# Decoder layer on one core: the first tokens per tile, the first scores earlier, and a new order of weight splits

## The reference

```python
x = x + attention(layernorm(x))           # 16 heads of 64, keys and values from the same tokens
x = x + cross_attention(layernorm(x), ctx)# 16 heads of 16, keys and values from ctx, masked
x = x + experts(layernorm(x))             # 8 experts 256 -> 512 -> 256, gelu, summed and gated
```

## Time and profile before

| | |
|---|---|
| median of 3 runs | 907.7 us |
| the profiled execution's own time | 908.18 us |
| its span | 906.4 us |
| TensorE busy | 861.6 us (95%) |
| ScalarE busy | 626.7 us (69%) |
| VectorE busy | 562.3 us (62%) |
| GpSimd busy | 308.7 us (34%) |
| granted TensorE clock, mean | 0.991 |

### The profile page before, as it was taken

One profiled execution on the slowest core, in us unless ns is written; L12 is line 12 of the kernel. 1 busy time (PEld: TensorE's weight loads), 2 busy tenths in 40 slices (PEclk: granted clock), 3 DMA queues, 4 the chain that ended last, 5 costly groups with the idle time before them and its releaser, 6 DMA issues.

```text
span 906.4 us, 18085 instructions
## 1 busy us (share of the span) xinstructions
PE 861.6 (95%) x6299; PEld 781.1 (86%) x6299; DVE 562.3 (62%) x1167; ACT 626.7 (69%) x1772; POOL 308.7 (34%) x355
## 2 busy tenths in 40 slices
PE   8899999999999987999998799999999999999997
PEld 6798989989998976888888689999999999999996
DVE  5788898888889866787887755454223322332223
ACT  4988888888887865989898956754454445444542
POOL 4564564445455658465755520000000000000000
PEclk9999999999999997999999999999999999999999
DMA  5410000000000027555455113310000000000000
GB/s 179 146 41 1 2 1 1 2 1 2 1 25 1 2 55 184 127 149 132 103 140 140 48 52 102 94 34 24 1 1 1 24 0 0 0 24 1 1 1 24
DMA packets 21792, 42.29 MB, mean 47 GB/s; under 512 B 3144, under 2 KB 3152, under 8 KB 21712
## 3 DMA queue, kind: packets, MB, share of 16 engines
q1 hardware_dynamic: 21120, 40.91, 16.5%
q10 hardware_dynamic: 592, 0.34, 0.2%
HBM read 30.75 MB, written 10.49 MB: 45 GB/s over the span
## 4 chain that ended last, share of the span: by engine, by line
PE 71%; DVE 11%; ACT 11%; issue 4%; DMA 2%; POOL 1%; SPq 0%; DVEq 0%; ACTq 0%; POOLq 0%
PE Y L562 24%; PE A L562 22%; PE S L562 14%; ACT probs L949 6%; PE T L677 3%; DVE arena L1112 2%; PE O L562 2%; DVE nm L1143 2%; DVE PT L1038 2%; PE O L694 2%; DVE arena L1038 1%; PE O L697 1%; ACT PT L957 1%; DMA stage<-arena 1%; PE S L655 1%
## 5 line engine op out<-in xcount | busy, mean ns | idle before, releaser
L1038 DVE TENSOR_TENSOR PT<-probs,PT 128x512 fp32r<-128x512 f32 x128 | 90.0, 703 | 231.0 <-ACT PT L1018 231.0
L562 PEld LDWEIGHTS Y<-arena,PT 128*128 128x128 f32 x1536 | 199.9, 191 | 11.4 <-DVE PT L1038 1.4
L562 PE MATMUL Y<-arena,PT 128*128 128x256 f32 x1536 | 204.0, 283 | 0.4
L949 ACT ACTIVATE probs<-S,nm 128x128 f32<-128x128 f32 x512 | 181.0, 371 | 30.2 <-DVE nm L1143 28.1
L1382 POOL TENSOR_TENSOR probs<-probs,rinv 128x512 f32<-128x512 f32 x128 | 133.2, 1041 | 173.6 <-DVE rinv L1148 173.5
L562 PE MATMUL A<-XT,arena 128*128 128x512 f32 x612 | 160.4, 396 | 1.4 <-DVE arena L1112 1.1
L1018 ACT ACTIVATE PT<-probs 128x512 fp32r<-128x512 f32 x128 | 80.8, 631 | 101.7 <-PE Y L562 101.3
L562 PEld LDWEIGHTS A<-XT,arena 128*128 128x128 f32 x612 | 107.9, 189 | 21.8 <-DVE arena L1112 4.3
L949 ACT ACTIVATION_READ_ACCUMULATOR probs<-S,nm 128x1 f32 x512 | 107.5, 210 | 0.0
L1038 DVE TENSOR_TENSOR PT<-T,PT 128x512 fp32r<-128x512 f32 x128 | 87.4, 683 | 23.4 <-ACT PT L957 21.5
L562 PE MATMUL S<-XT,arena 128*128 128x512 f32 x384 | 99.9, 395 | 0.0
(11 more groups left out here) (134 smaller groups left out, 1424.0 us busy)
## 6 DMA issues: line engine op xcount, KB each, us to landing
wst<-in_pieces SPq DMA_DIRECT2D x52, 256.0 KB, 2.6
stage<-arena SPq DMA_DIRECT2D x32, 256.0 KB, 2.3
arena<-stage SPq DMA_DIRECT2D x48, 128.0 KB, 3.9
arena<-stage SPq DMA_DIRECT2D x24, 256.0 KB, 3.9
xs<-in_x SPq DMA_DIRECT2D x4, 512.0 KB, 4.1
craw<-in_ctxT SPq DMA_DIRECT2D x4, 512.0 KB, 3.9
out<-craw SPq DMA_DIRECT2D x4, 512.0 KB, 2.6
rowc<-in_rows ACTq DMA_DIRECT2D x1, 264.0 KB, 5.4
```

What stands on the lines that cost most here:

```text
L562: mm = pe.matmul(acc, lhs[a], rhs[b], start=first and i == 0, stop=last and i == 2, skip_group_check=shared)
L949: last = act.activation(probs[:, n % 4, u * P:(u + 1) * P], S[n % 2][:, u * P:(u + 1) * P], ACT.Exp, bias=nm[:, n % 4, u:u + 1], accum_out ...
L1038: dve.tensor_tensor(out_, src, hi.bitcast(F32), ALU.subtract).then_inc(sem_, 1)
```

## The change

Six edits, all in the opening of the first attention:

1. The first 512 tokens come in four DMAs of one tile each, two issued by SyncE ahead of the weights and two by ScalarE ahead of its small loads. VectorE takes each tile's statistics when that tile is there.
2. TensorE transposes tile t into the first bank as soon as tile t is normalised, and no longer after all four.
3. `QK_OPEN` and `V_OPEN`: slot 4 holds the projections of K and Q of chunk 0 (jobs 0 and 1), and V tile 0; slot 5 V tile 1; slots 5 and 6 no further Q or K; slot 7, after `scores` 0, V tiles 2 and 3 and K and Q of chunk 1. V tiles 0 and 1 keep banks A1 and O; tiles 2 and 3 now share bank A1, and both are evacuated only when tile 3 is done. From slot 8 on the order on TensorE is the old one.
4. `weight_slots`: the splits in slots 4 to 15 are put in another order and later slots, so also the loads. Slots 4 to 7 hold three instead of seven of them, slots 8 to 15 nine instead of six (slots 8 and 10 two each instead of one, slot 13 one instead of none), and slot 2 of the second group one instead of none.
5. `LOW_BY_DVE`: VectorE takes the rests of pieces 0 and 2 in slot 4 (was 2), of 4 in slot 7 (was 5), of 8 in slot 11 (was 7), of 12 in slot 14 (was 10).
6. The sum of the experts' biases (`sum_b2`, two small matmuls and a copy on ScalarE) moves from slots 5 and 6 to 8 and 9.

The diff, without the lines that only carry these through:

```diff
+        QK_OPEN = {4: (0, 1), 7: (2, 3)}
+        V_OPEN = {4: (0,), 5: (1,), 7: (2, 3)}
...
+                    if opening(g) and v < 8:
+                        jobs = (QK_OPEN if name == "qk" else V_OPEN).get(v, ())
+                        return [(i, BOTH) for i in jobs]
...
-            return {(0, 0): (1,), (0, 1): (0,), (0, 2): (2,), (0, 4): (4,), (0, 5): (5, 6), (0, 6): (8, 3),
-                    (0, 7): (9, 10), (0, 8): (7,), (0, 9): (12,), (0, 10): (13,), (0, 11): (14,),
-                    (0, 12): (11,), (0, 14): (15,), (1, 4): (16,), (1, 6): (17,), (1, 8): (18,),
+            return {(0, 0): (1,), (0, 1): (0,), (0, 2): (2,), (0, 4): (5, 6), (0, 6): (4,),
+                    (0, 8): (3, 9), (0, 9): (10,), (0, 10): (8, 7), (0, 11): (13,), (0, 12): (14,),
+                    (0, 13): (12,), (0, 14): (11,), (1, 2): (15,), (1, 4): (16,), (1, 6): (17,), (1, 8): (18,),
                     (1, 10): (19,)}.get((g, n), ())
...
-        LOW_BY_DVE = {(0, 0): (1,), (0, 2): (0, 2), (0, 5): (4,), (0, 7): (8,), (0, 10): (12,), (1, 5): (16,)}
+        LOW_BY_DVE = {(0, 0): (1,), (0, 4): (0, 2), (0, 7): (4,), (0, 11): (8,), (0, 14): (12,), (1, 5): (16,)}
...
-            tokens(0)
+            for t in range(2):
+                sp.dma_start(xs[:, t:t + 1, :], x[0][:, t:t + 1, :]).then_inc(x_tile[t], 16)
...
+                        if by_tile and k == 0:
+                            if t < TILES - 1:
+                                pe.wait_ge(ln_tile, t + 1)
+                            else:
+                                pe.wait_ge(ln_x, nth(GRP, ph, g, 0))
...
-                if ph == 0 and opening(g) and n == 5:
+                if ph == 0 and opening(g) and n == 8:
                     pe.wait_ge(b2_split, 2)
...
+            for t in range(2, TILES):
+                act.dma_start(xs[:, t:t + 1, :], x[0][:, t:t + 1, :]).then_inc(x_tile[t], 16)
             act.dma_start(bias[:, :], biases).then_inc(b_in, 16)
...
-                act.wait_ge(v_ps, nth(VJ, ph, g, job))
+                act.wait_ge(v_ps, nth(VJ, ph, g, 3 if ph == 0 and opening(g) and job == 2 else job))
```

More of the change, by code:

```diff
@@ L178, in build @@
         H = (A0, A1, S0, S1)
-        x_in = [sem("x_in0"), sem("x_in")]
+        x_tile = [sem(f"x_tile{t}") for t in range(TILES)]
+        x_in = sem("x_in")
+        ln_tile = sem("ln_tile")
         b_in = sem("b_in")
@@ L426, in bank_qk, with acc_v @@
             return bank1(g, job)
-        def bank_v(g, job):
-            return {1: O, 2: T}.get(job, A1) if opening(g) else A1
+        def acc_v(g, job):
+            if opening(g) and job == 1:
+                return O[:, 0:D]
+            return A1[:, D:2 * D] if opening(g) and job == 3 else A1[:, 0:D]
         PE_ORDER = (
@@ L618, in project_v @@
                 if ph == 0:
-                    if not (opening(g) and job < 3):
-                        pe.wait_ge(v_lo, nth(VJ_F1, ph, g, 0 if opening(g) and job == 3 else job - 1))
+                    if opening(g) and job == 2:
+                        pe.wait_ge(v_lo, nth(VJ_F1, ph, g, 0))
+                    elif not (opening(g) and job < 4):
+                        pe.wait_ge(v_lo, nth(VJ_F1, ph, g, job - 1))
                     if job == 0:
@@ L624, in project_v @@
                         pe.wait_ge(xp_lo, xpe(0, g + 1, 3))
-                    i, src, bank = 4 * (job // 4) + 2, tokens_t(ph, g), bank_v(g, job)
-                    tiles = [(job % 4, 0)]
+                    i, src = 4 * (job // 4) + 2, tokens_t(ph, g)
+                    tiles = [(job % 4, acc_v(g, job))]
                 else:
@@ L1067, in ln_apply @@
                                              ALU.subtract, ALU.mult)
+                    if ph == 0 and opening(g) and t < TILES - 1:
+                        last.then_inc(ln_tile, 1)
                 if tiles[-1] == TILES - 1:
@@ L1184, in stats @@
             def stats(ph, g, tiles):
-                if ph == 0:
-                    dve.wait_ge(x_in[not (isinstance(g, int) and g == 0)],
-                                16 if isinstance(g, int) and g == 0 else (GROUPS - 1) * 16)
-                else:
+                first = ph == 0 and opening(g)
+                if ph == 0 and not first:
+                    dve.wait_ge(x_in, (GROUPS - 1) * 16)
+                elif ph > 0:
                     dve.wait_ge(x_ready, nth(GRP, ph - 1, g, 0))
```

26 lines of the change are left out of this document (14 added, 12 removed).

## The result

| | before | after |
|---|---|---|
| median | 908.17 us (906.2 to 909.7, 20 runs) | 910.13 us (907.3 to 911.8, 19 runs) |
| the profiled execution's own time, span | 908.18, 906.4 us | 907.29, 905.5 us |
| its mean granted clock | 0.991 | 0.993 |
| its first projection, scores 0, scores 2, scores 8 at | 12.89, 19.95, 31.03, 60.23 | 11.73, 17.22, 28.79, 59.30 |

The ratio is 1.0018 (95% interval 1.0011 to 1.0025): the kernel became slower by 1.6 us by this ratio (1.96 us by the medians), while 0.65 us of gain was forecast. It lies within the 0.3% taken as no change, but the median is above the upper end of the range, 909.0. One more execution of the changed kernel took 4312.69 us and is left out of the 19 as a slow one. Two later measurements of the unaltered changed kernel gave 1.0004 (0.9996 to 1.0013) and 1.0014 (1.0003 to 1.0025).

A forecast was written before the change was run, and what follows sets the result against it. TensorE, busy 95%, bounds the kernel; late tokens and a 3.30 us wait with slow clock can be won. Gain 2.5 at scores 2 less 1.85 given back is 0.65 us: 907.1 us, range 904.2 to 909.0.

The forecast's parts named there:

- Step 1: First token loads and statistics: normalisation ends at 9.0 instead of 9.91, gain 0.9 us; 10.3 if tiles land at 6.2.
- X: End of the token normalisation, in times of the old trace: 9.91 us before, forecast 9.0.
- Small loads are slow: Rival at the first token loads: four DMAs land at up to 6.2, X = 10.3, time 908.4 us; chance 0.07.
- Step 2: From X to the first projection: 2.98 us down to 2.4, so 11.4; gain together 1.5 us.
- Step 3: From first projection to scores 0: start at X + 8.35 = 17.35 instead of 19.95, gain 2.6 us.
- The meeting: Before scores 0, VectorE's rests of pieces 0 and 2 and GpSimd's splits alternate; without it scores 0 at X + 7.3.
- VectorE first: Rival before scores 0: VectorE's rest of piece 0 starts before GpSimd's split, scores 0 at X + 7.3, 906.0 us; chance 0.17.
- Step 4: Scores 0 to scores 2: 11.08 to 11.2 us, waits of 1.15 and 1.5 replacing 3.30, clock 1.00; gain at scores 2 2.5.
- the clock falls all the same: Rival after V tile 4: clock halves, 1.6 us lost, gain 0.65 becomes a loss of 1.0, 908.7 us; chance 0.11.
- Step 5: Slots 10 to 13 and the next group's slot 2: added roundings, bias copy and VectorE rest give back 1.85 us.
- The 0.35 us for the second group: Term of step 5: slot 2 of the next group gets one rounding more, of which 0.3 was idle; costs 0.35 us.
- Later splits find room: Rival in the later slots: step 5 costs nothing, 905.2 us, or 904.2 with VectorE first; chance 0.27.

The follow-up runs named there:

- splits evened: Changed kernel with the weight splits of slots 8 to 10 spread over slots 7 to 10, VectorE's rest of piece 8 in slot 10: 907.55 us, ratio 0.9991.
- filling the waits alone: Changed kernel with unread matmuls on ones in TensorE's two waits around V tile 4: 908.71 us, ratio 0.9999 to the kernel before.
- shortening them alone: Changed kernel with VectorE taking the rests of V tiles 2, 3 and K of chunk 1 ahead of the maximum of scores 1: 907.29 us, ratio 0.9976.

## Why the prediction was wrong

**Step 1, X at 9.0: right within 0.3 us in two profiles and 0.6 late in the third, partly for another reason.** The last statistic ended at 5.61, not 4.5, so the inverse root started at 6.5; the rest of piece 1, at 6.34, was earlier than before (6.84). In the first profile GpSimd's inverse root decided (0.92 us of waiting) and X was 9.33 (7.95 + 1.38). It was 8.72 in the second, and 9.57 in the third, where the rest of piece 1 decided as forecast, but started only at 7.58. "Small loads are slow" is out. The Trainium skill's advice to prefer one DMA to several (SBUF — State Buffer, Summary: rules for kernel authors) is for transfers that DMA bounds; the four loads here landed 2.4 to 3.5 us after issue, the one before after 3.9.

**Step 2, first projection at X + 2.4 = 11.4: right.** 11.73 in the first profile, that is X + 2.40; X + 2.66 and X + 2.39 in the others.

**Step 3, scores 0 at 17.35: right in the first profile, partly by luck, short in others.** 17.22, with the alternation that was assumed; but from the first projection it is 5.49 us where the sum has 5.95, which made up for the X that was 0.33 late. From the first projection to scores 0 it is 5.5 us in the four profiles of this opening where VectorE gets in between, and 6.3 in the four where GpSimd is served twice first. The meeting was seen, but only two orders of it were thought of, and both had VectorE's first rest no later than second. The third costs 0.8 to 0.85 us.

It is also the one that comes with VectorE's row first. In the five profiles where GpSimd's row starts 0.11 to 0.16 us ahead, VectorE gets in between; in the five where VectorE's starts 0.05 to 0.30 ahead, it is served last. So the condition of the rival "VectorE first" ("if its rest of piece 0 starts before GpSimd's split") came true in half of the profiles, with the opposite effect. By the rule that step 3 cites, the instruction issued second blocks; the rows with VectorE ahead don't bear that out, at least not by the starts that they record. Why it is so, no run shows: a VectorE row starts 0.08 us before the end of the one ahead of it, so that in one of the five GpSimd may have been first all the same, and no experiment moved one start alone.

**Step 4, scores 2 at 28.55 at full clock: this is the step that failed.** Its waits were right (1.15 and 1.5 forecast, 1.01 and 1.23 measured) and so, nearly, was scores 2 in the first profile, 28.79: K of chunk 2 and the bias sum take 1.60 and 0.43 us where the sum has 1.39 and 0.25. What failed is that the clock stays up. The rival "the clock falls all the same" had the place (right behind V tile 4), the sign and nearly the price (1.6 forecast; scores 0 to scores 2 takes 1.33 more), and got a chance of 0.11. "A burst of work stands in the middle" was the reason against it: 0.8 us of V tile 4 between 1.01 and 1.23 us of waiting did not prevent the fall in half of the executions or more (25 of 42 by the mean clock). It was also no either-or: the same program does both. The Trainium skill (TensorE: Matmul & The Clock Gate, Part 1: The HAM clock gate) says that the stretches over which activity is judged run freely and don't start with the kernel, so that the point where the clock changes varies from run to run. That two profiles of the same waits differ agrees with it; no run here was made to test it.

**Step 5, 1.85 us handed back: right in kind, too large.** 30.5 - 29.2 (or 29.5) is 1.0 to 1.3 us up to scores 8, where the sum has 1.5, and the evened splits give 1.1 of it back. They move one rounding out of slot 10 and VectorE's rest of piece 8 out of slot 11, so which of these two terms costs how much isn't separated; the double rounding does stand in ScalarE's row ahead of PT. The 0.35 us for the second group can't be told from the spread: from scores 8 to phase 1 it is 288.3 and 288.6 us before, 288.7 to 289.0 after.

**The sum.** Forecast lead 2.5 - 1.85 = 0.65. In the first profile it is 2.24 at scores 2, 0.93 at scores 8 and 0.45 where phase 1 starts: that execution is what was forecast. That it is 0.9 again in the whole span is luck of phase 1 (168.72 against 169.10 us). In the second and third, scores 2 came at 30.64 and 31.18, so of the lead over 31.03 and 31.66, 31.35 in the mean, 0.2 to 0.7 us is left, and the slots then take 1.1: slower than before.

What the slow clock cost before was no offset: next to nothing at 3.4 us. At 6.8 us it does cost 1.2; by the mean clocks at most two fifths of the executions of the kernel before have that. Executions with the high clock lie at 908.5, 908.7 and 909.3 us where the kernel before has 908.17, 909.26 and 909.3; so even these lie between 0.3 us above and 0.6 below it. That GpSimd goes first in part of them would explain that (in "splits evened" it does so at a high clock), but isn't shown for these executions. Which share each of the two has in the median isn't separated, since both profiles with the fall also had GpSimd first and a longer phase 1; but filling the waits alone, and shortening them alone, removed all the low clocks.

Put into the sum, the prices found bring the lead to about nothing: 0.65 as forecast, 0.75 more because the slots cost 1.1 and not 1.85, less 0.65 for the clock and 0.4 for the order (each in half of the executions), less 0.4 for the two terms of step 4. The three measurements show a loss of 0.4 to 1.6 us; why it is more than nothing stays open.

The rivals: the order meant by "VectorE first" (its rest done first, GpSimd's splits behind) appears in no profile. "Later splits find room" is refuted by the evened splits.

## What to carry to other kernels

When a long wait is cut into shorter ones, look at the clock in several executions: two waits of 1.0 and 1.2 us around 0.8 us of work still lost it in about half of them, and a single profile showed the other half. Compare two profiles part by part, too, and not by their spans: a part that the change doesn't touch differed by up to 1.6 us. Ask too what hides a slow clock: 3.4 us of it behind a wait for VectorE cost nothing before, and in the new order, with nothing to hide it, 1.3 us. Then move what the waiting engine waits for ahead of what it doesn't (VectorE's rests ahead of a maximum), and don't pay for an early start by crowding later slots: of 2.2 us won at scores 2, 1.1 to 1.3 went in the next slots, which had no room. A forecast from one profile should say which of the operations that meet at one moment could go the other way, and price each order.
